# One exponential for the two heads of a pair, and GpSimd's two-input operations in halves, in a two-layer transformer kernel on one core

## The reference, cut to what matters

```python
att = jnp.einsum('bhqd,bhkd->bhqk', q, k) * scale
causal = jnp.tril(jnp.ones((t, t), dtype=bool))
att = jnp.where(causal, att, -jnp.inf)
att = jax.nn.softmax(att, axis=-1)
y = jnp.einsum('bhqk,bhkd->bhqd', att, v)
...
z = z - jnp.max(z, axis=-1, keepdims=True)      # entmax15: a chain of small operations on 16 logits per token
zs = -jnp.sort(-z, axis=-1)
...
```

## Time and profile before

| | us |
|---|---|
| median of 3 runs (lowest, highest) | 2663.76 (2661.55, 2675.57) |
| the profiled execution's own time | 2670.14 |
| its span, first to last instruction | 2667.7 |
| TensorE busy | 2407.9 (90%) |
| VectorE busy | 2035.3 (76%) |
| ScalarE busy | 1869.8 (70%) |
| GpSimd busy | 1034.1 (39%) |

### The profile page before, as it was taken

How to read it: one execution, slowest core, us unless ns; L and a number is a source line. 1 busy time by engine, 2 the same in 40 slices (tenths; PEclk the granted TensorE clock), 3 DMA queues, 4 the chain that set the end, 5 groups by cost and what they waited for, 6 DMA issues and landing times.

```text
span 2667.7 us, 68317 instructions
## 1 busy us (share of the span) xinstructions
PE 2407.9 (90%) x24861; PEld 829.7 (31%) x24861; DVE 2035.3 (76%) x5616; ACT 1869.8 (70%) x3804; POOL 1034.1 (39%) x1710
## 2 busy tenths in 40 slices
PE   6889799999999998999989899999999999889784
PEld 3323232333323332333322333233323333233222
DVE  4884688867978688886977869977787958785772
ACT  3578477787668777787667777787677767667472
POOL 2323452344524363253522545334542535253221
PEclk8899799999999999999999999999999999999797
DMA  6211232223222243122321233212332132121211
GB/s 198 78 50 51 82 94 62 83 79 115 88 71 73 68 129 100 58 79 78 113 84 50 70 95 121 72 61 93 109 108 64 62 93 91 47 88 40 85 60 62
DMA packets 192539, 220.40 MB, mean 83 GB/s; under 512 B 36912, under 2 KB 143824, under 8 KB 192208
## 3 DMA queue, kind: packets, MB, share of 16 engines
q1 hardware_dynamic: 192208, 215.97, 26.2%
HBM read 113.07 MB, written 101.71 MB: 81 GB/s over the span
## 4 chain that ended last, share of the span: by engine, by line
PE 65%; DVE 17%; ACT 6%; issue 4%; DMA 4%; POOL 1%; SPq 1%; ACTq 0%; DVEq 0%; POOLq 0%
PE ps L1227 26%; PE ps L1348 16%; PE ps L1290 8%; PE ps L1329 8%; DVE mx L1888 6%; ACT probs L1624 4%; DVE ps L1885 3%; PE ps L1234 2%; PE ps L1304 1%; DMA stk_k<-k 1%; PE ps L1315 1%; DVE st L1852 1%; DVE x L1902 1%; ACT xn L1576 1%; PE ps L1388 1%
## 5 line engine op out<-in xcount | busy, mean ns | idle before, releaser
L1624 ACT ACTIVATE probs<-ps 128x512 f32<-128x512 f32 (+2 forms) x2560 | 1248.3, 559 | 457.4 <-PE ps L1329 449.9
L1888 DVE TENSOR_REDUCE mx<-ps 128x1 f32<-128x512 f32 (+2 forms) x1536 | 897.0, 639 | 193.1 <-PE ps L1290 107.2
L1885 DVE CUSTOM_DVE_ANT_0 ps<-ps,mask_b 128x512 f32<-128x512 f32 (+1 forms) x1024 | 613.4, 652 | 198.6 <-PE ps L1290 194.8
L1785 POOL TENSOR_SCALAR_AFFINE_SELECT probs<-probs 128x256 f32<-128x256 f32 (+1 forms) x768 | 369.4, 485 | 917.7 <-ACT probs L1624 915.8
L1348 PE MATMUL ps<-probs,vaug 128*17 128x512 f32 (+3 forms) x6144 | 615.6, 510 | 8.5 <-POOL probs L1785 3.3
L1290 PE MATMUL ps<-stk_k,stk_q 48*128 48x512 f16 (+3 forms) x3072 | 457.6, 337 | 97.2 <-DMA stk_k<-k 27.9
L1329 PE MATMUL ps<-stk_q,stk_k 50*128 50x512 f16 (+3 forms) x3072 | 455.1, 333 | 71.9 <-DVE mx L1888 28.5
L1329 PEld LDWEIGHTS ps<-stk_q,stk_k 50*128 50x128 f16 x3072 | 137.2, 94 | 520.9 <-issue 370.9
L1290 PEld LDWEIGHTS ps<-stk_k,stk_q 48*128 48x128 f16 x3072 | 140.4, 94 | 474.5 <-issue 339.0
L1227 PE MATMUL ps<-turned,wqkv 128*32 128x512 f32 x2048 | 268.3, 607 | 8.1 <-ACT turned L1563 2.7
L1348 PEld LDWEIGHTS ps<-probs,vaug 128*17 128x17 f32 x6144 | 142.7, 98 | 301.2 <-issue 212.3
(11 more groups left out here) (165 smaller groups left out, 2388.9 us busy)
## 6 DMA issues: line engine op xcount, KB each, us to landing
o<-oT SPq DMA_DIRECT2D x128, 256.0 KB, 2.4
stk_q<-q SPq DMA_DIRECT2D x256, 96.0 KB, 2.4
stk_k<-k SPq DMA_DIRECT2D x128, 192.0 KB, 3.6
q<-parts SPq DMA_DIRECT2D x64, 256.0 KB, 2.1
k<-parts SPq DMA_DIRECT2D x64, 256.0 KB, 2.1
yT<-o SPq DMA_DIRECT2D x64, 256.0 KB
inverse<-inverse_sums SPq DMA_DIRECT2D x64, 256.0 KB
stk_k<-k SPq DMA_DIRECT2D x128, 96.0 KB, 2.4
```

What stands on the lines that cost most here:

```text
L1624: act.activation(probs[:, step % PBUF, heads, cols], src, ACT.Exp, scale=exponent[l])\
L1785: pool.affine_select(out=diag, in_=diag, compare_op=ALU.is_ge, fill=0.0, base=0, pattern=[[0, k], [1, P]], channel_multiplier=-1).then_inc ...
L1885: dve.tensor_tensor_reduce(tile, tile, mask_b[:, BANK - width:BANK], 1.0, LOWEST, ALU.add, ALU.max, most)\
L1888: dve.tensor_reduce(most, tile.rearrange("q (k w) -> q k w", k=k), AX.X, ALU.max)\
```

## The change: one ACTIVATE for a pair, halves on GpSimd, and a new order

Three things change together.

First, `exponentials` issues one ACTIVATE for both heads of a pair. Its input runs over two neighbouring PSUM banks, so a pair must lie in two banks that follow each other in the hardware: `take_two` picks among the five such places (`ADJACENT`). Both banks are read out by one instruction and hence share one semaphore value (`RELEASE`, `BEFORE`), the second bank's tiles being told free by the first bank's semaphore.

Second, GpSimd's five kinds of 128x512 two-input operation run as two instructions of 256 columns each.

Third, the planner knows of it: the cost of a pair's exponential is one term, a wait for two neighbouring free banks is added, VectorE's small operations with two inputs are charged up to 0.35 us each where GpSimd is planned to be busy (`port_time`), entmax steps may be held back while GpSimd's planned queue is long (`quiet_time`), and all but a few rows of `RULES` hold other weights. So the order of the whole program changes.

```diff
@@ planner
+TWO_INPUTS = {"logit": 3, "ent": {1: 2, 2: 0, 3: 2, 4: 4, 5: 7, 6: 3}, "gate": 4, "stat": 2, "ao": 1, "fo": 1}
+PORT = 0.35
...
+    def port_time(self, item, time):
+        two = TWO_INPUTS.get(item[0], 0)
+        if item[0] == "ent":
+            two = two[item[3]]
+        return min(max(0.0, self.busy["POOL"] - max(self.busy["DVE"], time)), two * PORT)
+
+    def quiet_time(self, step, rule):
+        return self.busy["POOL"] - rule.quiet if step[0] and step[0][0][0] == "ent" else 0.0
...
+    def pair_bank_time(self):
+        return min(max(self.free[i], self.free[i + 1]) for i in ADJACENT)
+
+    def take_two(self, first, second):
+        i = min(ADJACENT, key=lambda i: max(self.free[i], self.free[i + 1]))
+        self.hold(first, i)
+        self.hold(second, i + 1)
+        self.released[i + 1] = self.released[i]
+        self.freed[i + 1] -= 1
+        self.release[second] = self.release[first]
+        return i, i + 1
...
-        time = max(self.rows[u], self.st_time(2))
+        time = max(self.rows[u], self.st_time(2), self.pair_bank_time())
...
-        banks = [self.take(("st", u, j, h, r)) for r in range(2)]
+        banks = self.take_two(("st", u, j, h, 0), ("st", u, j, h, 1))
         self.run("st", start, n * ((z - a) / 2400 + 0.006))
+        end = self.on("ACT", self.pe + HOP, 0.17 + 2 * n * (z - a) / 1200)
         for b in banks:
-            end = self.on("ACT", self.pe + HOP, 0.17 + n * (z - a) / 1200)
...
-    (2, 0.4, 2, 3.4, 9, 6.96, 3.12, 7.04, 3.78, 7.42, 2.1, 0.83, 2, 1.5, 5, 1.36),
+    (3, 0, 2, 4.13, 9, 6.96, 3.12, 8.58, 3.78, 10.65, 1.69, 0.88, 2, 1.5, 4.87, 1.19, 9),
...
@@ ScalarE
-                for r in range(2):
-                    src = arrived(act, ("st", u, j, h, r))[:, 0:k * (z - a)].rearrange("q (k w) -> q k w", k=k)
-                    heads = slice(2 * h + r, 2 * (h + k), 2)
-                    act.activation(probs[:, step % PBUF, heads, cols], src, ACT.Exp, scale=exponent[l])\
-                        .then_inc(read_out(("st", u, j, h, r)), 1)
+                written(act, ("st", u, j, h, 1))
+                b = BANKS[PLACE["st", u, j, h, 0][0]]
+                src = ps[:, BANK * b:BANK * (b + 2)].rearrange("q (r n) -> q r n", r=2)[:, :, 0:k * (z - a)]
+                dst = probs[:, step % PBUF, 2 * h:2 * (h + k), cols]
+                if k > 1:
+                    src, dst = src.rearrange("q r (k w) -> q r k w", k=k), dst.rearrange("q (k r) w -> q r k w", r=2)
+                act.activation(dst, src, ACT.Exp, scale=exponent[l]).then_inc(read_out(("st", u, j, h, 1)), 1)
...
@@ GpSimd
+            def in_halves(out, one, two, op):
+                for half in range(2):
+                    cols = slice(HALF_BANK * half, HALF_BANK * (half + 1))
+                    ins = pool.tensor_tensor(out[:, cols], one[:, cols], two[:, cols], op)
+                return ins
...
-                pool.tensor_tensor(q, q, cos[:, BANK * key[2]:BANK * (key[2] + 1)], ALU.mult).then_inc(cos_ready, 1)
+                in_halves(q, q, cos[:, BANK * key[2]:BANK * (key[2] + 1)], ALU.mult).then_inc(cos_ready, 1)
```

More of the change, by code:

```diff
@@ L40 @@
 HALF = P // 2
+HALF_BANK = BANK // 2
 PAIRS = HG // 2
@@ L67 @@
 BANKS = (0, 1, 2, 3, 4, 6, 7)
+ADJACENT = [i for i in range(len(BANKS) - 1) if BANKS[i + 1] == BANKS[i] + 1]
 SETUP_BANKS = 5
@@ L291, in __init__ @@
         self.free, self.used, self.place = [0.0 if b >= SETUP_BANKS else NEVER for b in BANKS], [0] * len(BANKS), {}
+        self.freed, self.released, self.release, self.before = [0] * len(BANKS), [None] * len(BANKS), {}, {}
         self.ring, self.st, self.stepped, self.steps, self.pvs, self.held = [], [], 0, {}, [], []
@@ L350, in take, with hold @@
         b = self.free.index(min(self.free))
+        self.hold(key, b)
+        return b
+    def hold(self, key, b):
         self.place[key] = (b, self.used[b])
@@ L353, in take @@
         self.free[b] = NEVER
-        return b
+        self.before[key] = self.released[b]
+        self.freed[b] += 1
+        self.released[b] = self.release[key] = (b, self.freed[b])
+    def pair_bank_time(self):
[8 more added lines that the diff above has]
+        return i, i + 1
     def st_time(self, n=1):
@@ L381, in give @@
             for engine, length in rest:
+                if engine == "DVE":
+                    length += self.port_time(item, time)
                 time = self.on(engine, time, length + extra_time(item))
@@ L568, in score_work @@
     return sum(2 * (packed(dict(score_parts(i))[p]) * dict(score_parts(i))[p] / 1000 + 0.12) for _, _, i, _, p in score_items(u))
-Rule = namedtuple("Rule", "feed_dve feed_act fed fed_st st s late due pair chain stay pace lead spread ahead_dve ahead_act")
+Rule = namedtuple("Rule", "feed_dve feed_act fed fed_st st s late due pair chain stay pace lead spread ahead_dve ahead_act quiet")
 RULES = [Rule(*values) for values in (
[27 rows of a table removed]
[27 rows of a table added]
 )]
@@ L649, in program_order @@
                 step = plan.head(n)
-                if step and not takes_time(step) and plan.ready[n] <= plan.pe:
+                if step and not takes_time(step) and max(plan.ready[n], plan.quiet_time(step, rule)) <= plan.pe:
                     plan.give(n)
@@ L671, in program_order @@
             if time is not None and not takes_time(plan.head(n)):
-                choices.append((time, 9, "wait", ()))
+                choices.append((max(time, plan.quiet_time(plan.head(n), rule)), 9, "wait", ()))
             elif time is not None:
@@ L723, in program_order @@
     PLACE.update(plan.place)
+    RELEASE.update(plan.release)
+    BEFORE.update(plan.before)
     return order[:last + 1] + [("flag",)] + order[last + 1:]
@@ L741 @@
 EARLY = True
-PLACE = {}
+PLACE, RELEASE, BEFORE = {}, {}, {}
 FINISH = []
@@ L1017, in read_out @@
         def read_out(key):
-            return drained[PLACE[key][0]]
+            return drained[RELEASE[key][0]]
         def in_sbuf(eng, key):
-            b, n = PLACE[key]
-            eng.wait_ge(drained[b], n + 1)
+            b, n = RELEASE[key]
+            eng.wait_ge(drained[b], n)
         def parts_in_dram(eng, o):
@@ L1207, in claim @@
             def claim(key):
-                b, n = PLACE[key]
-                if n:
+                if BEFORE[key]:
+                    b, n = BEFORE[key]
                     pe.wait_ge(drained[b], n)
-                return t_bank[b], full[b]
+                return tile(key)
             def tile(key):
@@ L1774, in part2 @@
                 pool.wait_ge(part0_ready, PART0[key] + 1)
-                pool.tensor_tensor(parts[:, o % PRING, 1], qf[o % QRING], parts[:, o % PRING, 0], ALU.subtract)\
-                    .then_inc(parts_ready, 1)
+                in_halves(parts[:, o % PRING, 1], qf[o % QRING], parts[:, o % PRING, 0], ALU.subtract).then_inc(parts_ready, 1)
             def causal(u, j, h):
```

6 lines of the change are left out of this document (3 added, 3 removed), and 52 rows, old and new, of the table RULES.

## The result

The changed kernel takes 2760.3 us at the median (2757.6 to 2768.1), the kernel before 2662.7 in the same session: a ratio of 1.036, 95% interval 1.0328 to 1.0391. It is 3.6% slower. The forecast was 2647 us with a range of 2612 to 2684, so direction and range both failed.

What follows compares the result with a forecast made beforehand. TensorE, busy 90% of the span with many short holes, was taken as the bound. Terms -6 - 4 + 2 - 3 + 2 - 8 = -17 us on the profiled 2670.1 gave 2653, or 2647 against the median; range 2612 to 2684.

Steps and rivals of the forecast that it cites:

- The cost of the exponential: On ScalarE: one instruction over 1024 columns takes 1025 ns, a pair ends some 60 ns sooner, 77 us less busy time.
- What it gives: Effect of the single exponential on the end time, from the exponentials' 4% of the chain: -6 us, bounds -29 and +26.
- The upper bound: Worst case of the single exponential: each of 62 waits grows as the first bank comes free 0.42 us later, +26 us.
- The halves: GpSimd's two-input operations in halves: -4 us from shorter VectorE stalls, +2 us for GpSimd's extra instructions.
- The order: The new program order: three terms of -3, +2 and -8 us on TensorE's waits.
- the counts of who had a bank last: Old waits of the score products, priced by changed counts of a bank's previous holder: -14, +7, +7 and -3, sum -3 us.
- the weighing that follows its scores more closely: TensorE's weighing of values comes sooner after its last score product, cover thin at 77 of 768 weighings: +2 us.
- stalls that the plan now knew: Order planned with 60 us of VectorE stalls known: a tenth of 75.5 us of waits, -8 us, bounds -38 and +20.
- The pairs' waits for exponentials: Score-with-keys pairs taking a bank after another exponential, 1695 times instead of 1265: 21.5 us x +0.34, +7 us.
- Rival B: Pairs wait for two adjacent free banks, 0.62 us each; 80 more waits give +33, 2697 us; slower; chance 0.17.
- "At the claim of the first bank nothing is new": Argument against slower pairs in TensorE's score-with-keys products: both banks were waited for before the first product anyway.

Runs made afterwards that it cites:

- e1: The changed kernel, same order and banks, but one exponential for each bank again, each bank released by itself: 2754.4 us, ratio 1.0324 to the kernel before.
- e5: The kernel before, same order, GpSimd whole, one exponential per pair, banks chosen so that neighbours stay free: 2827.8 us, ratio 1.0597.
- e6: Same order and banks as e5, but two exponentials for a pair and a release for each bank: 2810.8 us, ratio 1.0534.
- e9: The kernel before, same order, GpSimd in halves, neighbouring banks where free, one exponential for 657 of 1280 pairs: 2811.3 us, ratio 1.0552.
- e11: Same order, halves and banks as e9, but two exponentials for every pair: 2800.1 us, ratio 1.0498.
- e3: The kernel before with GpSimd's 384 two-input operations in halves and nothing else: 2658.9 us, ratio 0.996.
- e7: The changed kernel's order with two exponentials for a pair and every bank chosen anew, neighbours or not: 2732.6 us, ratio 1.0268.
- e10: The changed kernel's planner without the wait for neighbours, two exponentials in any two banks, halves, stalls charged, weights searched anew: 2668.2 us, ratio 1.0005.

## Why the prediction was wrong

**The cost of the exponential: right.** 1025 ns forecast, 1023 measured. ScalarE's busy time was forecast at about 1793 us and came to 1803.5, 66 us less than before instead of 77.

**What it gives: too much.** -6 forecast. In the new order it costs 6 by the medians and 10 by the ratios (e1 against the changed kernel, within the intervals), at e5 and e6 17, and at e9 and e11 14 by the ratios, with half of the pairs fused. The upper bound, the first bank held for 0.42 us longer (+26), was the nearer one: the chain's 4% counted how long exponentials lay on the path and not when a bank came free.

**The halves: right in sign, and larger alone.** -4 + 2 forecast, -11 measured with the old order (e3), and nothing seen with the new. The remaining excess was forecast as 42 us and is 46.9 in e3; the estimate that was off in it was the number of stalls, taken as constant or as doubling, which went from 72 to 106.

**The order: this is the step that failed.** The sum had -3 for it from the counts of who had a bank last, +2 for the weighing that follows its scores more closely, and -8 for stalls that the plan now knew, together -9. Measured by e1 against e3, order and banks together cost about 97 us (1.0324 against 0.996), of which 15 come back when the banks are freed in the same order (e7).

Two terms were mis-sized above all. The pairs' waits for exponentials had +7, from 21.5 us and a count that rose by a third; they came to +46.8, since waits became not a third but 2.6 times as many (48 to 126). The weighing had +2, by its 3.3 us of waits for GpSimd; its waits for exponentials and GpSimd went from 4.9 to 29.2 us (1.6 + 3.3 to 20.1 + 9.1), and its products are busy for 20.8 us more. The prediction had seen that the cover was thin at 77 of 768 weighings and priced it by the old waits all the same.

Each price was that of waits in the old trace, multiplied by a ratio of counts. Such a price takes for granted that the share of claims that must wait stays as it was. But an order is fitted to its rules, and with a new rule that share changed, at the weighing too, which claims no bank of a pair. The waits for VectorE did fall, as the count for the pairs said, and by more than the sum had (75.5 to 54.0). The sign there was right, and it weighed little. TensorE's time without work, forecast at some 243 us, came to 318.0.

**Rival B named one half of the mechanism** and its mark, waits of L1364 for L1662 above 50 us (68.3). It priced each wait more at 0.62 us, which gives 78 x 0.62 = 48 us against 46.8 measured at that line. That is not all net: the pairs' waits for VectorE fell by 17.2 us (41.7 to 24.5), so about 35 of the 88 us lie at the pairs. The 44 at the weighing no rival had. "At the claim of the first bank nothing is new" was the wrong comfort: what is new is which banks may be claimed. B's 2697 us was 63 below the measured time, its chance of 0.17 was too low, and the range ended at 60 such waits. What an order longer by itself could cost was bounded at +20.

**What was not looked at.** The program's planner keeps a clock for the whole order, and the prediction doesn't use it. It ends at 2589.9 us before and at 2693.5 after, +104; on the chip it was +98. In the six kernels whose order and banks both came from a planner the chip ended 43 to 74 us after that clock, so differences of some 30 us in it say nothing (e10), and one of 100 does.

TensorE's 29.7 us more of busy time are not explained by a run; 20.8 of them are at the weighing. The mean granted clock of the profiled execution fell from 0.956 to 0.953, which would make 8 us by an estimate from these two and the 2407.9 us of before. It isn't the whole: e11 is busy for 2431 us at a clock of 0.959. The busy time is what overlapping products cover together, so products that no longer overlap their neighbours would count more. That is argued, not shown.

## What to carry to other kernels

When an instruction is widened over two buffers, count first what the demand for the pair does to the choice of buffers, then what the instruction saves: here some 60 ns saved 1280 times gave nothing, and an order planned for neighbours was 3.6 to 4.4% slower. In a tight pool take the buffer that has been free longest, even if no plan asks for it: in the old order its slack was worth 5%. A forecast that multiplies the waits of an old trace by counts failed here where the order changed. An order found by a search belongs to the rules it was searched for, so a change of rules is to be compared with an order searched as long, and each part of such a change is worth its own run with the order held still.

## What the runs showed of the hardware

- One ACTIVATE streams over the border of two PSUM banks at the rate of one: 1023 ns for 1024 columns against 601 for 512, 812 for 768, 596 for 512 in two banks of 256.
- Small VectorE operations (4 to 64 columns) that start beside a two-input GpSimd operation of 512 or 256 columns can be held until it ends. In the trace before some 70 of them started after the GpSimd operation and ended 0.02 to 0.28 us after its end. The longest of two lines went from 1258 to 775 ns and from 1317 to 732 as GpSimd's operation went from 1275 to 730. Halving the holder cut the sum of stalls by 28% (49.1 to 35.5 us) and not by half.
- GpSimd hardly waits for VectorE: what its operations take above their medians, where that is over 60 ns, adds up to 1.8 us before and 2.3 after, with 384 instructions more.
